# Two LSTM chains half a round apart, with the first cells written by VectorE

## The reference

```python
h = relu(layernorm(x))
h = relu(einsum('ts,bsh->bth', adj, h @ Wg0 + bg0))
h = relu(einsum('ts,bsh->bth', adj, h @ Wg1 + bg1))
for p in range(1, 5):                    # windows of p tokens
    last = lstm_last(Wih[p-1], Whh[p-1], b, windows of p tokens of h)   # gates i, f, g, o
    h[:, last token of each window] = last
x = x + h
f = relu(layernorm(x))
agg = einsum('nm,bmd->bnd', A_hat, f)    # A_hat: adj + I, scaled by the degrees
z = batchnorm(agg @ W1.T + b1)           # over all batches and tokens
x = x + batchnorm(relu(z) @ W2.T + b2)   # again over all
```

## Time and profile before

| | us |
|---|---|
| median of 3 runs | 639.04 |
| lowest, highest | 638.77, 639.62 |
| profiled execution | 635.4 |
| its span, first to last instruction | 633.5 |

### The profile page before, as it was taken

How to read it: one execution, slowest core, us unless ns; L and a number is a source line. 1 busy time by engine, 2 the same in 40 slices (tenths; PEclk the granted TensorE clock), 3 DMA queues, 4 the chain that set the end, 5 groups by cost and what they waited for, 6 DMA issues and landing times.

```text
span 633.5 us, 9027 instructions
## 1 busy us (share of the span) xinstructions
PE 529.4 (84%) x2769; PEld 452.0 (71%) x2769; DVE 448.2 (71%) x1033; ACT 329.7 (52%) x620; POOL 203.7 (32%) x308
## 2 busy tenths in 40 slices
PE   3679869988997699999958999999599989675656
PEld 3468748877995588989846899889377878454436
DVE  3454367888875688878566887884777887756776
ACT  3423535454555365555554656566456556245554
POOL 2340263202004652222054531310640220609952
PEclk9769979989799799999997999999899999796998
DMA  7210000100000201101021011010011101792007
GB/s 216 67 35 1 1 5 30 66 18 1 17 2 24 77 1 68 51 2 52 1 101 66 0 67 50 1 50 33 34 51 50 51 1 51 273 401 89 1 1 265
DMA packets 20075, 37.45 MB, mean 59 GB/s; under 512 B 1690, under 2 KB 6212, under 8 KB 20036
## 3 DMA queue, kind: packets, MB, share of 16 engines
q1 hardware_dynamic: 19332, 36.60, 16.2%
q10 hardware_dynamic: 704, 0.39, 0.2%
HBM read 22.30 MB, written 14.68 MB: 58 GB/s over the span
## 4 chain that ended last, share of the span: by engine, by line
issue 42%; PE 23%; POOL 16%; DVE 9%; POOLq 5%; ACT 4%; DMA 1%; DVEq 1%; ACTq 0%; SPq 0%
POOL z_back L391 4%; POOLq L321 3%; POOL y_post L323 3%; PE gate_ps L977 3%; PE gate_ps L979 3%; PE gate_ps L978 3%; POOL x_pre L323 3%; PE pre_ps L977 2%; PE pre_ps L978 2%; PE pre_ps L979 2%; POOL h L346 2%; PE post_ps L977 1%; PE post_ps L979 1%; PE post_ps L978 1%; POOLq L319 1%
## 5 line engine op out<-in xcount | busy, mean ns | idle before, releaser
L580 ACT ACTIVATE gate<-gate_ps,gate_bias 128x256 f32<-128x256 f32 (+2 forms) x312 | 163.8, 565 | 52.9 <-PE gate_ps L979 31.2
L977 PE MATMUL gate_ps<-by_class_hi,wih_hi 128*128 128x256 f32 (+2 forms) x264 | 88.8, 336 | 20.2 <-DVE by_class_lo L663 16.0
L596 ACT ACTIVATE gate<-cell 128x512 f32<-128x512 f32 (+2 forms) x88 | 45.2, 514 | 99.5 <-DVE cell L841 60.0
L978 PE MATMUL gate_ps<-by_class_hi,wih_lo 128*128 128x256 f32 (+2 forms) x264 | 87.0, 330 | 0.0
L979 PE MATMUL gate_ps<-by_class_lo,wih_hi 128*128 128x256 f32 (+2 forms) x264 | 86.9, 329 | 0.0
L977 PEld LDWEIGHTS gate_ps<-by_class_hi,wih_hi 128*128 128x128 f32 x264 | 52.5, 199 | 26.8 <-issue 15.0
L351 POOL TENSOR_TENSOR cell<-gate 128x512 f32<-128x512 f32 x16 | 20.6, 1288 | 147.7 <-ACT gate L580 142.9
L977 PE MATMUL gate_ps<-hstep_hi,whh_hi 128*128 128x256 f32 (+2 forms) x192 | 60.7, 316 | 0.0
L979 PE MATMUL gate_ps<-hstep_lo,whh_hi 128*128 128x256 f32 (+2 forms) x192 | 60.6, 316 | 0.0
L978 PE MATMUL gate_ps<-hstep_hi,whh_lo 128*128 128x256 f32 (+2 forms) x192 | 60.6, 315 | 0.0
L978 PEld LDWEIGHTS gate_ps<-by_class_hi,wih_lo 128*128 128x128 f32 x264 | 52.6, 199 | 4.2
(11 more groups left out here) (244 smaller groups left out, 1429.2 us busy)
## 6 DMA issues: line engine op xcount, KB each, us to landing
...
```

Source lines behind the costliest of these rows:

```text
L580: nc.scalar.activation(gate[:, chain, g, 0:size], gate_ps[k % GATE_BANKS][:, 0:size], ACT.Tanh if g == G_GATE else ACT.Sigmoid, bias=gate_ ...
L596: nc.scalar.activation(gate[:, chain, G_GATE, 0:size], cell[:, chain, 0:size], ACT.Tanh)\
L977: nc.tensor.matmul(ps, w[0], m[0], start=start, stop=False)
L978: nc.tensor.matmul(ps, w[1], m[0], start=False, stop=False)
```

## The change

The rounds are no longer loops with a common body: one list of 99 slots is written out. 11 slots are a half; there are nine halves. Even slots of a half have the first six steps of one chain, odd slots the last five steps of the other chain, so chain 1 runs half a round behind chain 0. In the first half the odd slots are empty, in the last half the even ones. Input and output units have fixed positions in a half, for the first and the second of two batches; a position below zero lies in the half ahead. The prologue does batches 0 and 1 whole and the statistics and norm of batch 2. Only batches 14 and 15 are left for the tail. The cell of p = 1 is written by DVE as in the other first steps (L823 of the new kernel), and so are the float32 states of the even tokens (L843), behind the low part. z is spilled and read back for eight batches instead of twelve, x1 for twelve instead of sixteen.

```diff
-TURNS = [(chain, *step) for step in STEPS for chain in range(CHAINS)]
+LEAD = 6
+HALF = len(STEPS)
+HALVES_RUN = CHAINS * ROUNDS + 1
+N_SLOTS = HALF * HALVES_RUN
+
+
+def step_in(slot):
+
+    half, pos = divmod(slot, HALF)
+    if pos % 2 == 0:
+        chain, r, s = half % 2, half // 2, pos // 2
+    else:
+        chain, r, s = (half + 1) % 2, (half - 1) // 2, LEAD + pos // 2
+    return (r, chain, s) if 0 <= r < ROUNDS else None
...
-PRE_TURN = {"stats": (1, 4, 7, 13), "norm": (3, 6, 10, 16),
-            AGG0: (4, 9, 13, 18), LIN0: (5, 10, 14, 19), LIN1: (6, 11, 15, 20), AGG1: (7, 12, 17, 21)}
...
+PRE_POS = {"stats": (-4, 3), "norm": (-2, 5), AGG0: (0, 6), LIN0: (1, 7), LIN1: (2, 8), AGG1: (3, 10)}
+POST_POS = {"turn": (0, 1), "agg": (5, 8), "hid0": (6, 9), "hid1": (7, 10), "norm": (4, 7), "stats": (2, 4)}
...
-DEG_SUM, DEG_TOKENS, DEG_POW, DINV_DIAG, DINV_ROWS = 3, 3, 4, 5, 7
-HAT_CHUNK = (8, 11, 14, 17)
+DEG_SUM, DEG_TOKENS, DEG_POW, DINV_DIAG, DINV_ROWS = 1, 1, 2, 3, 5
+HAT_CHUNK = (8, 10, 12, 14)
...
-                for n, (chain, p, step, sub, nb) in enumerate(TURNS[:POOL_CELLS]):
-                    pool.wait_ge(gates_act, at(r, N_GATES, GATES_BEFORE[n] + 2))
-                    nc.gpsimd.tensor_tensor(cell[:, chain, :], gate[:, chain, I_GATE, :],
-                                            gate[:, chain, G_GATE, :], ALU.mult).then_inc(cell_ready, 1)
-                    if n >= 1:
-                        even_tokens(n - 1)
...
+                else:
+                    dve.wait_ge(gates_act, k + 2)
+                    nc.vector.tensor_tensor(c_, i_, g_, ALU.mult).then_inc(cell_ready, 1)
...
+                elif p == 1:
+
+                    hi, lo = (part[:, chain, :].rearrange("h (t b) -> h t b", b=SUBS)[:, :, sub] for part in by_class)
+                    nc.vector.tensor_tensor(c_, o_, g_, ALU.mult).then_inc(h_done, 1)
+                    dve.wait_ge(h_done, g + 1)
+                    nc.vector.tensor_copy(hi, c_).then_inc(class_hi, 1)
+                    dve.wait_ge(class_hi, CLASS_AT[r, chain, 1, sub])
+                    low(lo, c_, hi).then_inc(class_lo, 1)
+                    if r > 0:
+                        dve.wait_ge(turn_mm, batch_of(r - 1, chain, sub) + 1)
+                    nc.vector.tensor_tensor(h32[:, chain, 0::2, sub], gate[:, chain, O_GATE, 0:T // 2],
+                                            gate[:, chain, G_GATE, 0:T // 2], ALU.mult).then_inc(even_done, 1)
```

More of the change, by code:

```diff
@@ L111, in later @@
-def later(r, more):
-    return not isinstance(r, int) or r > 0 or more > 0
-def class_count(chain, p, step):
-    return CLASS_AT[(chain, 1, SUBS - 1) if p == 2 else (chain, p, step)]
-def g_count(r, b):
-    return 8 * (b // 2) + 7 + b % 2 if isinstance(r, int) and r == 0 else at(r, N_PRE, 4 * b + 4)
+EARLY = SUBS
+PRE_POS = {"stats": (-4, 3), "norm": (-2, 5), AGG0: (0, 6), LIN0: (1, 7), LIN1: (2, 8), AGG1: (3, 10)}
+POST_POS = {"turn": (0, 1), "agg": (5, 8), "hid0": (6, 9), "hid1": (7, 10), "norm": (4, 7), "stats": (2, 4)}
@@ L916, in _ @@
+            last = range(BATCHES - SUBS, BATCHES)
+            for n in last:
+                turned(n, (pre_ps, post_ps)[n % 2])
+                stats_post(n)
+            for n in last:
+                normed(n, y_last[n % 2][:, :], nrm[n % 2], post_nhi, post_nlo)
+            for n in last:
+                agg_out(n, gate_ps[n % 2], n % 2)
+            for n in last:
                 for half in range(HALVES):
-                    hid_stats(rho, b, half)
+                    hid_stats(n, half)
```

747 lines of the change are left out of this document (343 added, 404 removed).

## The result

| | before | after |
|---|---|---|
| median, us | 638.9 (4 runs) | 655.95 (4 runs, 654.04 to 658.42) |
| profiled execution, us | 635.4 | 656.01 |
| its span, us | 633.5 | 654.2 |

The ratio is 1.027, 95% interval 1.023 to 1.031. The forecast was 644.8 us: the sign is right, the loss of 17 us is nearly three times the 5.9 us forecast.

A forecast was written before the change was run, and what follows sets the result against it. TensorE was taken as the bound (114.7 of 124.7 us busy in a full round), with DVE close. The stages 53 + 113 + 301 + 50 + 37 + 24 + 61 = 639 us, plus 5.5, gave 644.8 us, 0.9% slower; range 616 to 660.

The forecast's parts named there:

- the ramps: Halves 0, 1, 7 and 8, where the staggered chains fill and drain: forecast to cost +43 us.
- the steady halves: Halves 2 to 6, both chains running: 60.2 us each against 62.35 before, 301 us in all, a gain of 10.7.
- PE's content in a steady half: TensorE's work in one of halves 2 to 6: 55.1 us, half of 97.7 + 8.2 + 2.7 + 1.6 = 110.2 a round.
- half 1: Second half, without output work, with two of four hat chunks: DVE 51 us plus exposed waits of 3.
- Prologue, tail, half 8: First turn at about 53 us (-16.8); tail 24 us (-9.9); last half, one chain alone, 34 us plus 3 for the clock.
- The GpSimd work: The p = 1 products moved to DVE: 17 us more for DVE against 16 of slowdown given back, a draw.
- The walk's two long waits: Slot-by-slot walk through a half: PE waits 1.95 us before the input's second aggregation, 1.85 for the normalised output's low part.
- What lies around the span: Added to the 639.3 us span: 1.9 us for profiled execution and 3.6 for the runs' median, together 5.5.
- Rival 1: Steady halves: DVE keeps up and PE's content decides, 56.1 us a half, -20.5 us, 624 us in all; chance 0.32.
- Rival 3: Slots 2 to 5: GpSimd's norms block DVE, 3.4 us a half, +17 us, 662 us in all; chance 0.05.
- Rival 2: Steady halves or ramps: PE's clock falls, seven more spells, +15 us, 660 us; sign granted clock under 0.9; chance 0.09.
- Rival 4: Steady halves: the stagger does only half, 58.8 us a half, -7 us, 638 us in all, no change; chance 0.13.

The follow-up runs named there:

- e11_warm: Changed kernel with eight matmuls of constants in each empty slot of halves 0 and 8, to keep PE's clock up: 651.09 us.
- e13_end8: Kernel with halves 0 and 1 both mended (641.37 us), output units of batches 12 and 13 moved behind ready turns in half 8: 638.59 us.
- e1_before_dve: Kernel before the change, with only the p = 1 cells and even float32 states moved from GpSimd to DVE: 637.42 us, ratio 0.998.
- e2_after_pool: Changed kernel with the p = 1 cells and even states put back on GpSimd: 656.33 us.
- e3_hat_early: Changed kernel with the four hat chunks behind slots 5, 7, 9, 10 of half 0 instead of 8, 10, 12, 14: 649.17 us.
- e6_half0: Changed kernel with the even input batch's second aggregation behind slot 4 instead of 3, in half 0 alone: 647.91 us.
- e8_pe_light: Changed kernel without the third matmul of each product in the aggregations, work the result needs: 624.27 us.
- e9_dve_light: Changed kernel with three quarters of the layer norms' statistics left out on DVE, work the result needs: 649.14 us.
- e10_norm_light: Changed kernel with GpSimd normalising one of four chunks in each layer norm, work the result needs: 654.35 us.
- e4_spread: Changed kernel with four position entries moved: three sets of statistics, and the even input batch's second aggregation from slot 3 to 4: 657.84 us.
- e18_norm3: Kernel with mended halves 0, 1 and 8, degree sums behind slot 3, chunks behind 6 to 9; even output norm moved from slot 4 to 3: 635.05 us.
- e7_shift: Changed kernel with the steady halves' input units one slot earlier, and some statistics and norms moved earlier too: 671.04 us.

## Why the prediction was right in its sign and wrong in its size

The mechanism was right: the ramps cost more than the steady halves give back. Two terms of the sum were too small, PE's content in a steady half and half 1. Of the 15 us by which the span missed, 6.1 lie in the steady halves, 4.9 in half 1, 1.4 in half 0, 2.6 in half 7 and 1.2 in the closing stage; the tail gives 0.9 back.

- **Prologue, tail, half 8.** 53, 24 and 37 us forecast; 52.9, 23.1 and 36.9 measured. Half 8 was luck in part. Its 37 had 3 us for the clock, but at a clock of 1.00 the half takes 36.8 us (e11_warm), and it had no term for the units ahead of the last turn, whose move shortened halves 7 and 8 by 7.9 us (e13_end8).
- **The GpSimd work.** "A draw": shown from both sides (e1_before_dve, e2_after_pool) for the time, not for DVE's busy time, which rises by 1.9 us a round (e1_before_dve). The term that was off is the slowdown given back: in round 2 of the kernel before the four products take 1.37, 1.36, 1.00 and 0.68 us and the casts 0.85, 0.84, 0.84 and 0.57, some 3 us over 0.69 and 0.43 in a round, or 12 in all, where I took 16.
- **The steady halves, failed in size: 307.1 against 301 us.** The walk's two long waits were right: idle time is 4.45 us a half against 5.1. The term that failed is PE's content. I put 12.5 us for what lies ahead of 342 in the round, where the earlier trace rows have 17.0 us of busy time there, some of it at the lower clock; the halves at full clock are busy for 56.4 us, not 55.1. That is 6.5 us in five halves. Spells in halves 2 and 5 add 3.1, and the shorter idling takes 3.2 off.
- **The ramps, failed in size: 51 against 43 us.** Halves 0 and 1 took 119.3 us against 113, half 7 52.6 against 50, with PE busy for 43.4 us where I had 39. Half 0 was near its walk (58.4 against 57 us), but by luck, as far as the runs show: it contains the aggregation's block, which the prediction doesn't name, and takes 51.2 us without it. The step that failed most is half 1, "DVE 51 us plus exposed waits of 3" with two of the four hat chunks: it took 60.9 us, since a third chunk falls into it, PE waits 4.3 us for u_lo behind them, and the clock is 0.94; without those chunks it takes 51.6, with 1.3 us for u_lo (e3_hat_early). What the prediction also did not say is that some 17 of the 51 us are no price of a stagger. The aggregation's block (7.2 us, e6_half0) and the chunks (6.3, e3_hat_early) go by moving one unit and the four chunks, and the two halves then take 106 us, 7 below the forecast; half 8's units give 3.8 more (e13_end8).
- **What lies around the span.** I added 5.5 us (profiled execution and median of before), it was 1.8: the 3.7 us hid part of the miss of the span (654.2 against 639.3).
- **The rivals.** Rival 1 is dead: its halves of 56.1 us did not come, and even with 5.5 us less of PE's matmuls they average 58.1 (e8_pe_light). Its remedy, a DVE that keeps up, gains nothing either: 2.6 us less of DVE work a half left the halves as they were (e9_dve_light). Rival 3 is dead (e10_norm_light). Rival 2's sign, a granted clock under 0.9, did not come (0.97 to 1.00), but it is partly true: two of five steady halves had a spell, and the clock takes back part of every wait removed (e4_spread, e9_dve_light, e18_norm3). Rival 4's 58.8 us a half did not come either: the stagger gave 0.9 us a half, where the forecast had 2.15 and rival 4 had 3.5. "I am wrong in the ramps if halves 0 and 1 take less than 105 us" did not come to pass, but the mended 106 lie at that edge.

So the stagger is not a loss by nature: with its ramps mended it takes 638.6 us against 638.2, and 635.05 against 637.4 with one more entry moved. The kernel before was not tuned in the same way, so whether the stagger is worth anything against an equally tuned order is not shown. By the medians, 14.6 us of the loss are order in halves 0 and 1 and 2.8 order in half 8.

Open: why a removed wait comes back as a spell in some halves and not in others, and whether the 1.9 us for u_lo can go; both tries (e4_spread, e7_shift) only moved it.
